# One scale-and-shift instruction folded away in a feed-forward layer norm, with the first turn of each group reordered

## The reference, cut to what matters

```python
def ffn_layer(x, g, bln, W1, b1, W2, b2):
    mu = x.mean(-1, keepdims=True)
    var = ((x - mu) ** 2).mean(-1, keepdims=True)
    xn = (x - mu) / jnp.sqrt(var + 1e-05) * g + bln
    hg = xn @ W1 + b1
    a, gate = jnp.split(hg, 2, -1)
    return a * jax.nn.gelu(gate, approximate=False) @ W2 + b2
for i in range(DEPTH):
    x = attn_layer(shift_tokens(x), Wqkv[i], q_scale[i], k_scale[i], Wo[i]) + x
    x = ffn_layer(shift_tokens(x), ln_g[i], ln_b[i], W1[i], b1[i], W2[i], b2[i]) + x
```

## Time and profile before

| | |
|---|---|
| Median of three runs | 2876.72 us (2874.08 to 2881.6) |
| Span of the profiled execution | 2876.3 us |
| PE busy | 2709.0 us (94%) |
| DVE busy | 2616.4 us (91%) |
| ACT busy | 2273.1 us (79%) |
| POOL busy | 2115.9 us (74%) |
| Granted PE clock, mean | 0.988 |

### The profile page before, as it was taken

How to read it: one execution, slowest core, us unless ns; L and a number is a source line. 1 busy time by engine, 2 the same in 40 slices (tenths; PEclk the granted TensorE clock), 3 DMA queues, 4 the chain that set the end, 5 groups by cost and what they waited for, 6 DMA issues and landing times.

```text
span 2876.3 us, 92923 instructions
## 1 busy us (share of the span) xinstructions
PE 2709.0 (94%) x36417; PEld 2060.1 (72%) x36417; DVE 2616.4 (91%) x3375; ACT 2273.1 (79%) x3824; POOL 2115.9 (74%) x1529
## 2 busy tenths in 40 slices
PE   8799978999999999999999999999999999999996
PEld 7577756777777777777777777777777777777774
DVE  6899968999999999999999999999999999999993
ACT  5799857878787887878788887878888787877873
POOL 5766658777778777777777787777777777877771
PEclk9899999999999999999999999999999999999998
DMA  1000013222223232232232233222322322322222
GB/s 57 23 2 2 1 36 76 70 71 65 71 63 76 71 76 64 66 78 67 67 76 68 66 74 73 69 67 68 75 68 66 78 65 63 72 67 58 63 66 78
DMA packets 103719, 178.41 MB, mean 62 GB/s; under 512 B 29350, under 2 KB 52708, under 8 KB 103396
## 3 DMA queue, kind: packets, MB, share of 16 engines
q1 hardware_dynamic: 102372, 174.60, 25.0%
q10 hardware_dynamic: 1152, 1.20, 0.1%
HBM read 22.62 MB, written 2.10 MB: 9 GB/s over the span
## 4 chain that ended last, share of the span: by engine, by line
POOL 26%; issue 24%; DVE 15%; PE 11%; ACT 5%; DMA 2%; POOLq 0%; DVEq 0%; SPq 0%; ACTq 0%
POOL spare L1454 15%; DVE spare L1285 5%; POOL pr L1492 4%; DVE qk_t L1294 3%; POOL spare L1463 3%; PE pa L843 3%; DVE ss L1278 3%; PE px L872 3%; DMA kT<-spare 2%; POOL xs_lo L1440 2%; DVE oT_lo L1354 1%; PE pg L982 1%; PE pg L930 1%; PE px L917 1%; POOL w_lo L1485 1%
## 5 line engine op out<-in xcount | busy, mean ns | idle before, releaser
L1454 POOL TENSOR_TENSOR spare<-spare,qk_t 128x1024 f32<-128x1024 f32 x384 | 910.2, 2393 | 11.5 <-POOL xs_lo L1440 8.1
L843 PE MATMUL pa<-w_hi,xs_hi 128*128 128x512 f32 x1152 | 511.8, 444 | 27.5 <-issue 8.4
L1470 POOL TENSOR_TENSOR sm<-sm,inv 128x512 f32<-128x512 f32 x192 | 201.8, 1051 | 446.7 <-DVE sm L1316 372.7
L1294 DVE TENSOR_TENSOR qk_t<-pa,rot 128x1024 f32<-128x1024 f32 x384 | 464.4, 1210 | 1.9 <-ACT spare L1048 1.7
L1285 DVE TENSOR_TENSOR spare<-pa,rot 128x1024 f32<-128x1024 f32 x384 | 464.5, 1210 | 0.0
L1278 DVE TENSOR_REDUCE ss<-spare 128x16 f32<-128x1024 f32 x384 | 457.5, 1191 | 6.7 <-ACT spare L1041 5.9
L843 PE MATMUL pa<-w_hi,xs_lo 128*128 128x512 f32 x1152 | 456.7, 396 | 0.0
L843 PE MATMUL pa<-w_lo,xs_hi 128*128 128x512 f32 x1152 | 454.9, 395 | 0.0
L872 PE MATMUL px<-ident_sb,spare 128*128 128x128 f32 x3072 | 409.0, 276 | 22.3 <-POOL spare L1463 11.6
L1463 POOL TENSOR_TENSOR spare<-spare,inv 128x1024 f32<-128x1024 f32 x192 | 365.9, 1906 | 80.6 <-ACT inv L1080 75.7
L872 PEld LDWEIGHTS px<-ident_sb,spare 128*128 128x128 f32 x3072 | 341.6, 141 | 111.0 <-issue 59.0
(11 more groups left out here) (180 smaller groups left out, 5970.0 us busy)
## 6 DMA issues: line engine op xcount, KB each, us to landing
kT<-spare SPq DMA_DIRECT2D x384, 256.0 KB, 3.7
pT<-prT SPq DMA_DIRECT2D x768, 64.0 KB, 2.0
w_part<-in_Wqkv SPq DMA_DIRECT2D x40, 192.0 KB, 3.7
wo<-in_Wo SPq DMA_DIRECT2D x6, 512.0 KB, 5.4
c_h<-in_x SPq DMA_DIRECT2D x4, 512.0 KB, 9.0
spare<-in_x SPq DMA_DIRECT2D x8, 256.0 KB, 5.0
out<-spare SPq DMA_DIRECT2D x8, 256.0 KB, 2.5
wo<-in_W SPq DMA_DIRECT2D x6, 341.0 KB, 5.2
```

Source lines behind the costliest of these rows:

```text
L843: last = pe.matmul(pa[(u + c) % 2][:, half * 512:half * 512 + 512], x[:, j * P:(j + 1) * P], w[:, at], start=(k == 0), stop=(k == 2))
L1294: dve.tensor_tensor(halves(qk_t[:, c, :]), halves(pa[(3 * j + c) % 2][:])[:, :, ::-1, :], table.unsqueeze(1).to_broadcast([P, HEADS, 2, DH ...
L1454: pool.tensor_tensor(qk_r[:, c, :], qk_r[:, c, :], qk_t[:, c, :], ALU.add)\
L1470: pool.tensor_tensor(keys(sm[:]), keys(sm[:]), over(inv[:, j % 2, 0, :], S), ALU.mult)\
```

## The change

The scale g is applied where ACT copies the centred values to `fc`, as a per-partition scale. `normalise` writes its product into PSUM tile `pg` in place. `scale_shift` is gone. ACT makes `fn_hi` from `pg` with the shift as a per-partition bias, and DVE makes `fn_lo` with one instruction that adds the shift to `pg` and subtracts `fn_hi`.

The orders change too. On ACT, the `shift_hi` of turn 0 moves from behind `copy_qT` to the end of the turn. On DVE, `normalise` moves ahead of the sum of squares of k in turn 0. The reciprocal becomes a step of its own; in turns 0 to 2 it comes after `rest_of_outputs`, in turn 3 it stays right behind the sum.

```diff
--- before.py
+++ after.py
@@ -667,7 +667,7 @@
             sq_q sq_k sum_q sum_k floored ln_done inv_ready
             cos_q cos_k sin_q sin_k rot_q rot_k norm_k tq_done tq_out tk_done tk_out v_out
             masked scores_done top_done sub_done scaled exp_done den_done rden_done probs_done turned pT_loaded pv_done pv_out oT_lo_ready wo_hi_ready wo_lo_ready
-            wo_done res_attn fs_ready center_done fc_ready fsq_ready var_done fln_done frs_ready fn_mul fn_ready fn_hi_ready fn_lo_ready w1_loaded w1_hi_ready w1_lo_ready
+            wo_done res_attn fs_ready center_done fc_ready fsq_ready var_done fln_done frs_ready fn_mul fn_hi_ready fn_lo_ready w1_loaded w1_hi_ready w1_lo_ready
             turned_out x_loaded added stored gate_done gate_out a_done h_ready w2_done res_ready""".split()
         s = {n: sem(n) for n in names}
 
@@ -1162,9 +1162,10 @@
                 def copy_centred(i, back):
                     g, live = group(i, back)
                     if live:
+                        act.wait_ge(s["ffn_loaded"], (g // GROUPS + 1) * FFN_DMAS * 16)
                         act.wait_ge(s["center_done"], g + 1)
                         wait_for(act, s["fn_mul"], g)
-                        act.copy(fc[:], pg[:]).then_inc(s["fc_ready"], 1)
+                        act.activation(fc[:], pg[:], ACT.Identity, scale=ln_par[:, 0:1]).then_inc(s["fc_ready"], 1)
 
                 def log_variance(i, back):
                     g, live = group(i, back)
@@ -1178,20 +1179,12 @@
                         act.wait_ge(s["fln_done"], g + 1)
                         act.activation(pg[:], fx[:], ACT.Exp, scale=-0.5).then_inc(s["frs_ready"], 1)
 
-                def scale_shift(i, back):
-                    g, live = group(i, back)
-                    if live:
-                        act.wait_ge(s["ffn_loaded"], (g // GROUPS + 1) * FFN_DMAS * 16)
+                def round_normed(i, back):
+                    g, live = group(i, back)
+                    if live:
                         act.wait_ge(s["fn_mul"], g + 1)
-                        act.activation(fx[:], fx[:], ACT.Identity, scale=ln_par[:, 0:1], bias=ln_par[:, 1:2])\
-                            .then_inc(s["fn_ready"], 1)
-
-                def round_normed(i, back):
-                    g, live = group(i, back)
-                    if live:
-                        act.wait_ge(s["fn_ready"], g + 1)
                         wait_for(act, s["a_done"], 3 * g)
-                        act.copy(fn_hi[:], fx[:]).then_inc(s["fn_hi_ready"], 1)
+                        act.activation(fn_hi[:], pg[:], ACT.Identity, bias=ln_par[:, 1:2]).then_inc(s["fn_hi_ready"], 1)
 
                 def round_w1(l):
                     act.wait_ge(s["w1_loaded"], 16 * (l + 1))
@@ -1227,8 +1220,6 @@
                             tables(i, 2, GELU)
                             gate_gelu(i, 2, 0)
                         copy_qT(i, j, 1)
-                        if j == 0:
-                            shift_hi(i, 0, 1)
                         if j == 2:
                             shift_hi(i, -1, 0)
                         if j == 1:
@@ -1249,13 +1240,12 @@
                         copy_oT(i, j, 3)
                         floor_norms(i, j, 0)
                         copy_v(i, j, 0)
-                        if j == 0:
-                            scale_shift(i, 2)
                         log_norms(i, j, 0)
                         if j == 2:
                             round_part(l, g)
                         if j == 0:
                             round_normed(i, 2)
+                            shift_hi(i, 0, 1)
 
                 act.preload_act_table_set(EXP_LN)
                 act.wait_ge(s["xs_zeroed"], 2)
@@ -1321,6 +1311,10 @@
                     if live:
                         dve.wait_ge(s["exp_done"], n + 1)
                         dve.reduce_sum(den[:], keys(pr[:]), AX.X).then_inc(s["den_done"], 1)
+
+                def reciprocals(i, j, back):
+                    n, j, live = tile(i, j, back)
+                    if live:
                         dve.wait_ge(s["den_done"], n + 1)
                         wait_for(dve, s["probs_done"], n)
                         dve.reciprocal(rden[:], den[:]).then_inc(s["rden_done"], 1)
@@ -1339,13 +1333,14 @@
                     if live:
                         dve.wait_ge(s["fc_ready"], g + 1)
                         dve.wait_ge(s["frs_ready"], g + 1)
-                        dve.tensor_tensor(fx[:], fc[:], pg[:], ALU.mult).then_inc(s["fn_mul"], 1)
+                        dve.tensor_tensor(pg[:], fc[:], pg[:], ALU.mult).then_inc(s["fn_mul"], 1)
 
                 def rest_of_normed(i, back):
                     g, live = group(i, back)
                     if live:
                         dve.wait_ge(s["fn_hi_ready"], g + 1)
-                        dve.tensor_tensor(fn_lo[:], fx[:], fn_hi[:].bitcast(F32), ALU.subtract).then_inc(s["fn_lo_ready"], 1)
+                        dve.scalar_tensor_tensor(fn_lo[:], pg[:], ln_par[:, 1:2], fn_hi[:].bitcast(F32), ALU.add, ALU.subtract)\
+                            .then_inc(s["fn_lo_ready"], 1)
 
                 def rest_of_outputs(i, j, back):
                     n, k, live = tile(i, j, back)
@@ -1396,15 +1391,19 @@
                         subtract_maximum(i, j, 2)
                         times_sin(i, j, l, 1, "sq_k", "rot_k", "sin_k")
                         times_cos(i, j, l, 1, "sq_k", "tk_done", "cos_k")
+                        if j == 0:
+                            normalise(i, 2)
                         sum_squares(i, j, 0, 1, "sq_k", "sum_k")
                         if j == 3:
                             add_attention(i, 1)
-                        if j == 0:
-                            normalise(i, 2)
                         if j == 1:
                             gated(i, 2, 0)
                         denominators(i, j, 2)
+                        if j == 3:
+                            reciprocals(i, j, 2)
                         rest_of_outputs(i, j, 3)
+                        if j < 3:
+                            reciprocals(i, j, 2)
                         if j == 1:
                             gated(i, 2, 1)
                         if j == 0:
```

More of the change, by code:

```diff
@@ L1179, in inverse_deviation @@
                         act.activation(pg[:], fx[:], ACT.Exp, scale=-0.5).then_inc(s["frs_ready"], 1)
-                def scale_shift(i, back):
-                    g, live = group(i, back)
-                    if live:
-                        act.wait_ge(s["ffn_loaded"], (g // GROUPS + 1) * FFN_DMAS * 16)
-                        act.wait_ge(s["fn_mul"], g + 1)
-                        act.activation(fx[:], fx[:], ACT.Identity, scale=ln_par[:, 0:1], bias=ln_par[:, 1:2])\
-                            .then_inc(s["fn_ready"], 1)
                 def round_normed(i, back):
@@ L1191, in round_normed @@
                     if live:
-                        act.wait_ge(s["fn_ready"], g + 1)
+                        act.wait_ge(s["fn_mul"], g + 1)
                         wait_for(act, s["a_done"], 3 * g)
-                        act.copy(fn_hi[:], fx[:]).then_inc(s["fn_hi_ready"], 1)
+                        act.activation(fn_hi[:], pg[:], ACT.Identity, bias=ln_par[:, 1:2]).then_inc(s["fn_hi_ready"], 1)
                 def round_w1(l):
```

## The result

| | before | after |
|---|---|---|
| Median | 2879.05 us (4 runs) | 2906.43 us (2903.33 to 2909.15, 4 runs) |
| Ratio | | 1.0101, 95% interval 1.0088 to 1.0114 |
| Span of the profiled execution | 2876.3 us | 2907.3 us |

What follows compares the result with a forecast made beforehand. It took the loop DVE to ACT to PE to DVE through turns 0 and 1 as what counts. 47 group distances x 0.4 = 19 us on the 2876.3 us span, plus 0.4, gave 2896 us; range 2846 to 2912.

Steps and rivals of the forecast that it cites:

- The sum's delay: Turn 0: normalise ahead of the sum of squares of k makes ACT's floor_norms begin 0.49 us later.
- `shift_hi`'s lost cover: ACT, turn 0: its 0.86 us now stand behind the wait, making square_q of turn 1 0.70 us late.
- Turn 1: First GELU 0.70 us late, second 0.53, DVE's sine of k 0.20, gated 0.35.
- The period: Next group starts 0.24 to 0.53 us later; 0.4 taken, near PE's side, because scores end VectorE's wait.
- The base: The median of the runs was put 0.4 us above the profiled span of 2876.3 us.
- The folding: Scaled copy 0.69 us, rounding step 0.59, fn_lo 0.73; ACT saves about 0.54 us per group, DVE 0.42.
- Rival A: VectorE's cut counts and square_k does not stall it: 0.59 us per group gained, 2849 us; chance 0.25.
- The reciprocal: DVE, turns 0 to 2: behind rest_of_outputs it saves 0.11 us per turn, 0.33 per group.
- the price of 0 for POOL: POOL gets the reciprocal 0.97 us later, but DVE's transpose of the result comes late enough to cost nothing.
- Rival C: Late reciprocal and copy_oT hold POOL's norm_probs, then turn_probs: 28 us on top, 2924 us; chance 0.07.
- the forecast's margin: Turns 1 and 2: DVE's 1.42 us before the transpose against POOL's 1.38 us to deliver its result.

Runs made afterwards that it cites:

- E2: The kernel after with normalise back behind the sum of squares of k on VectorE; 2884.36 us, ratio to before 1.002.
- E7: E3 with normalise ahead of the sum of squares of k on VectorE; 2873.66 us, ratio to before 0.9976.
- E1: The kernel after with shift_hi of turn 0 back behind copy_qT on ScalarE; 2872.23 us, ratio to before 0.9989.
- E4: The kernel before with only shift_hi of turn 0 moved to the end of ScalarE's turn; 2909.84 us, ratio 1.012.
- E9: The kernel before with only the second of shift_hi's two copies moved to the end of ScalarE's turn 0; 2893.48 us, ratio 1.0051.
- E3: The kernel before with the scale-and-shift folding alone, both engines' orders as before; 2855.58 us, ratio 0.9927.
- E6: E3 with the reciprocal behind rest_of_outputs in turns 0 to 2; 2851.97 us, ratio to before 0.9911.
- E5: The kernel after with the reciprocal right behind its sum in every turn again; 2906.76 us, ratio to before 1.009.

## Why the prediction was right

It forecast 2896 us, slower with a chance of 0.60, in a range of 2846 to 2912; 2906.43 was measured. The mechanism is the one forecast as far as `gated` in turn 1; the size was too small by a third, and how the delay reaches the next group was argued wrongly.

- *The sum's delay.* Forecast: `floor_norms` 0.49 late. Measured: 1519.42 - 12.34 = 1507.08, 0.56 late, with an idle wait of 0.61 us (forecast about 0.7). The 0.07 more is the step from the sum's end to `floor_norms`, 0.09 where 0.02 was taken. E2 and E7 show that the early `normalise` costs 18 to 22 us.
- *`shift_hi`'s lost cover.* Forecast: 0.86 us on the path. E1 and E4 show 32 to 34 us. Together, `square_q` was to be 0.70 late; it started at 1509.84, 0.75 late.
- *Turn 1.* The first GELU was 0.89 late (1512.52 against 1511.63), not 0.70. **This is the term that was mis-sized.** Of the missing 0.19, 0.05 comes with `square_q`, and 0.13 is the step from `square_q` to `inverse_norms`, 1.05 in place of 0.92, which the forecast had carried over by moving the GELU with `square_q`. The second GELU was 0.74 late (forecast 0.53) and the sine of k 0.41 late (forecast 0.20), held for 0.83 us. `gated` was 0.59 late (forecast 0.35).
- *The period.* Forecast +0.4 us, measured +0.645. PE's third gate block began at 1527.42 - 12.34 = 1515.08, 0.82 late, where 0.53 was forecast. PE's linear block, and not `square_k`, ends the last wait: by its own queue DVE would have reached `gated` at 1531.64 (its sum before it started at 1530.51, and that step was 1.13 before), the block ended at 1531.76 (1531.37 + 0.39), and `gated` started at 1531.80. From there VectorE's own queue carries the delay. As medians over the groups, lined up as in E9's table, `gated` is 0.57 late, the transpose behind turn 1 is 0.65 late, and every transpose from there to the next group's first is 0.65 or 0.66 late. The forecast set the next start near PE's 0.53, because VectorE waits for the scores at the start of turn 0. That wait did not grow (30.5 us before, 27.6 after), so this reason was wrong, and that 0.4 came as near as it did was partly luck: by DVE's own terms, 0.35 less 0.11, it would have been 0.24.
- *The base.* The forecast put the median 0.4 us above the profiled span, but these are different executions. In the runs where both are given, the time is 1.8 us above the span of the same execution (2909.15 and 2907.3).
- *The folding.* The step sizes held. Rival A, that VectorE's cut counts, is wrong for the change as made and right for E3.
- *The reciprocal.* Its 0.33 us per group did not come: E6 gained 4 us, which noise covers. The step did shrink as the rows said, from 0.71 to 0.59 (1519.25 to 1519.84), but POOL gets the reciprocal later, and VectorE's transpose waits for POOL about as long as was saved. The term was right for the instruction, and what failed is the price of 0 for POOL. By the rule of the Trainium skill ("VectorE: DVE Perf Modes", The DRAIN you can't avoid) this part would bring nothing, which is nearer to the time, but not for the rule's reason, since the step shrank.
- *Rival C* came true in part: behind turn 1 POOL waited 1.24 us, and the transpose started 0.16 late, where the forecast's margin was 0.04. E5 shows that this only cancels the saving and did not decide.

What stays open: why the second `xs_hi` copy in front of `square_q` makes `inverse_norms` start 0.13 us later (below).

## What to carry to other kernels

An instruction that "nobody needs soon" still has a place where it is free and places where it is not: it is free in front of a wait that would be there anyway, and costs most of its length behind it (33 us in E4, 0.70 us per group, for 0.85 us of copies). So for a move, first find the engine's next wait for another engine, and ask on which side of it the work stands. And an engine that is busy 79% on average can set the time of a stretch: look at busy shares per turn, not per launch.

## What the runs showed of the hardware that was not expected

- The time from one ScalarE instruction's start to the next one's is not fixed by the pair. `square_q` to `inverse_norms` took 1.05 us, with no wait shown, in the 46 groups of each kernel that has the second `xs_hi` copy right in front of `square_q`: the kernel after, E2, E4, E5 and E9. It took 0.90 to 0.92 wherever something else stands there, in the other turns of the same kernels too. Why is not shown.
- The rows of E9 show the same around that copy, which works on 64 partitions (64 to 127). It started 0.64 us after the rounding, 0.02 after the rounding's end, where `square_q` had started 0.52 after it, 0.10 before its end. `square_q` then started 0.02 after the copy's end, and `inverse_norms` 0.03 after the end of `square_q`. In the kernel after, the first of the two copies, on partitions 0 to 63, followed at 0.57 (1520.77 to 1521.34), 0.10 before the end of a rounding that is 0.05 longer.
- The old `fn_lo`, with two inputs in SBUF, took 691 to 1211 ns from group to group; the new one, with one input in PSUM, 657 to 752. The trace of before shows what the old one stood behind. In 46 of the 48 groups POOL's `norm_probs` was running when it started, and it ended 0.55 us after `norm_probs` ended, whatever its own start. In the 2 groups with nothing on POOL beside it, it took 691 and 692 ns. The new one took at most 752 with `norm_probs` beside it all along. The Trainium skill ("SBUF — State Buffer", SBUF: two separate sides) names such a cause: a VectorE instruction with two SBUF inputs shares a port with GpSimd, and the one that comes second is held until the other has ended. The trace agrees with this. So 0.36 us per group of the folding's gain (1110 to 749 ns) is in large part a wait for POOL that went.
